# Attention steps written out instead of looped, normalizer arithmetic moved off VectorE, and the first fold of ctx moved up GpSimd's queue

## The reference

```python
def _autocorrelation(Q, K, V):          # H = 8 heads, Q = layernorm(x), K = V = ctx
    qf = jnp.fft.fft(q, axis=2)
    kf = jnp.fft.fft(k, axis=2)
    corr = jnp.fft.ifft(qf * jnp.conj(kf), axis=2).real
    topk = int(C * np.log(L))           # 12 of 512 lags, for each channel
    w, idx = jax.lax.top_k(corr.transpose(0, 1, 3, 2), topk)
    w = jax.nn.softmax(w, axis=-1)
    for i in range(topk):
        g = jnp.minimum(idx[:, :, None, :, i] + pos, L - 1)
        out = out + w[:, :, None, :, i] * jnp.take_along_axis(v, g, axis=2)
x = x + _L0_xattn_ref(_layernorm(x), ctx, ctx)
x = x + _L0_ffn_ref(_layernorm(x), A_w, B_w, Wq_w, keys)
```

## Time and profile before

| | |
|---|---|
| median of 3 runs | 2534.56 us (2531.9 to 2537.17) |
| the profiled execution's own time | 2531.53 us |
| its span, first to last instruction | 2529.7 us |
| mean granted clock of PE | 0.967 of full speed |
| busy share of the span: PE, DVE, POOL, ACT | 92%, 72%, 62%, 37% |

### The profile page before, as it was taken

One profiled execution on the slowest core, in us unless ns is written; L12 is line 12 of the kernel. 1 busy time (PEld: TensorE's weight loads), 2 busy tenths in 40 slices (PEclk: granted clock), 3 DMA queues, 4 the chain that ended last, 5 costly groups with the idle time before them and its releaser, 6 DMA issues.

```text
span 2529.7 us, 32161 instructions
## 1 busy us (share of the span) xinstructions
PE 2317.3 (92%) x9728; PEld 1570.1 (62%) x9728; DVE 1821.3 (72%) x3961; ACT 944.4 (37%) x1727; POOL 1566.1 (62%) x1004
## 2 busy tenths in 40 slices
PE   3799998998998998998999999659999999999999
PEld 1456654654654564554556566348787887878877
DVE  3888887887887887887988878745555565555552
ACT  2344443344433533443453443323333333233331
POOL 4878877886887887886878887523333333333330
PEclk7899999999999999998999999779999999999999
DMA  5233232222322322322231122444444444444431
GB/s 189 92 104 109 71 103 97 84 71 92 120 71 71 129 83 71 109 103 71 71 137 59 61 102 100 156 149 150 167 150 158 158 157 161 162 149 166 149 133 50
DMA packets 111452, 289.80 MB, mean 115 GB/s; under 512 B 7168, under 2 KB 7296, under 8 KB 110208
## 3 DMA queue, kind: packets, MB, share of 16 engines
q1 hardware_dynamic: 111360, 288.81, 32.4%
HBM read 221.68 MB, written 67.11 MB: 114 GB/s over the span
## 4 chain that ended last, share of the span: by engine, by line
PE 54%; POOL 25%; issue 11%; DVE 5%; DMA 2%; ACT 2%; POOLq 0%; SPq 0%; DVEq 0%; ACTq 0%
POOL r_f L1220 7%; PE z L495 5%; PE out L495 5%; PE out L497 5%; PE z L497 5%; PE out L496 5%; PE z L496 5%; PE evac L512 3%; PE pair L525 3%; POOL vf L1216 3%; POOL half_fold L1212 3%; PE evac L536 3%; POOL half_fold L1213 3%; PE evac L537 3%; PE lag L569 3%
## 5 line engine op out<-in xcount | busy, mean ns | idle before, releaser
L1255 POOL TENSOR_TENSOR rows<-rows,cin 128x1024 f32<-128x1024 f32 x48 | 114.5, 2386 | 410.0 <-DMA rows<-out_dram 284.6
L1220 POOL TENSOR_TENSOR r_f<-prod 128x1024 f32<-128x1024 f32 x128 | 305.9, 2398 | 81.7 <-DVE prod L798 80.0
L597 PE MATMUL pair<-r_f,back 128*128 128x512 f32 x768 | 334.8, 592 | 0.0
L597 PEld LDWEIGHTS pair<-r_f,back 128*128 128x128 f32 x768 | 145.8, 190 | 170.1 <-issue 168.4
L569 PE MATMUL lag<-lags,p_f 128*128 128x256 f32 x1024 | 233.2, 381 | 12.9 <-DVE e L819 12.9
L495 PE MATMUL pair<-w_hi,wts_hi 128*128 128x512 f32 x512 | 211.1, 412 | 17.0 <-DVE prod L798 16.6
L569 PEld LDWEIGHTS lag<-lags,p_f 128*128 128x128 f32 x1024 | 193.0, 191 | 39.9 <-issue 13.8
L495 PE MATMUL out<-b_hi,zt_hi 128*128 128x512 f32 x512 | 208.0, 406 | 1.5 <-ACT zt_hi L1168 1.5
L495 PE MATMUL z<-a_hi,xt 128*128 128x512 f32 x512 | 207.8, 406 | 0.0
L496 PE MATMUL pair<-w_lo,wts_hi 128*128 128x512 f32 x512 | 202.0, 395 | 0.0
L497 PE MATMUL pair<-w_hi,wts_lo 128*128 128x512 f32 x512 | 201.7, 394 | 0.0
(11 more groups left out here) (141 smaller groups left out, 5490.9 us busy)
## 6 DMA issues: line engine op xcount, KB each, us to landing
vf<-in_ctx_dram SPq DMA_DIRECT2D x32, 1024.0 KB, 5.1
xf<-in_x_dram SPq DMA_DIRECT2D x32, 1024.0 KB, 5.8
out_dram<-att_sb SPq DMA_DIRECT2D x32, 1024.0 KB, 5.1
rows<-out_dram SPq DMA_DIRECT2D x64, 512.0 KB, 3.7
cin<-out_dram SPq DMA_DIRECT2D x64, 512.0 KB, 3.9
xin<-in_x_dram SPq DMA_DIRECT2D x64, 512.0 KB, 4.0
out_dram<-rows SPq DMA_DIRECT2D x64, 512.0 KB, 2.6
stat_in<-in_x_dram SPq DMA_DIRECT2D x28, 1024.0 KB, 7.2
```

What stands on the lines that cost most here:

```text
L597: return nc.tensor.matmul(pair_ps[:, bank, :], back[:, 3 * bank + n, :], r_f[:, row, :], start=n == 0, stop=n == 2)
L1220: nc.gpsimd.tensor_tensor(dst, prod[:, slot, 0:2, :], prod[:, slot, 2:4, :], ALU.add).then_inc(add_done, 1)
L1255: nc.gpsimd.tensor_tensor(half, first, second, op).then_inc(c_added, 1)
```

## The change

- `steps` no longer makes a loop. The 33 steps are written out on each engine, with constants in place of registers in semaphore waits and addresses.
- The normalizer: DVE keeps the four L729 and the reciprocal. Its three small arithmetic instructions L731, L732 and L740 go. ACT does the first two as Identity and Copy ahead of its root, and POOL adds the 1.5 from an array of constants, in place of one multiplication.
- `fold_v` is cut in two. Its first instruction runs right behind `fold_x`, ahead of the four sums into `r_f`; the other three stay at the end of the step.
- The transposes of `turn_weights` go to other banks: block 1 to a bank of `pair` instead of the `evac` bank that DVE's second L807 frees, so that the wait for L807 stands at block 3.
- Between the two parts, `add_x(0, 0, 0)` moves from the end of step 31 to step 32, behind `fold_w`.

```diff
-        def steps(eng, body):
-            for r in (1, 2, 3):
-                body(-1, r, True, r > 1, True, True)
-            with eng.Fori(0, B - 2) as k:
-                for r in range(4):
-                    body(k, r, True, True, True, True)
...
+        def steps(body):
+            for i in range(GROUPS + 1):
+                k, r = (i - 3) // GPB, (i - 3) % GPB
+                body(k, r, i < GROUPS, i >= 1, i + 1 < GROUPS, k + 2 < B)
...
-            return evac_ps[l][:] if l < 2 else pair_ps[:, l, :]
+            return (evac_ps[0][:], pair_ps[:, 2, :], pair_ps[:, 3, :], evac_ps[1][:])[l]
...
                         if l == 0 and a:
                             pe.wait_ge(evac_act, 6 * i + 6)
                         elif l == 1 and a:
+                            pe.wait_ge(prod_ready, prod_x(i, 1) + 1)
+                        elif l == 1:
+                            pe.wait_ge(att_done, i - 1)
+                        elif l == 3 and a:
                             pe.wait_ge(evac_dve, 2 * i + 2)
-                        elif l == 2 and a:
-                            pe.wait_ge(prod_ready, prod_x(i, 1) + 1)
...
-                nc.vector.tensor_scalar(y[:, :, 0], mv[:, :, 1], EPS, -0.5, ALU.add, ALU.mult).then_inc(norm_step, 1)
-                nc.vector.tensor_scalar(mv[:, :, 0], mv[:, :, 0], -1.0, None, ALU.mult).then_inc(norm_step, 1)
...
-                nc.vector.tensor_scalar(mv[:, :, 1], y[:, :, 1], 1.5, None, ALU.mult).then_inc(norm_step, 1)
...
             def root(m):
-                act.wait_ge(norm_step, 8 * m + 5)
-                nc.scalar.activation(norm_x[1][:, :, 1], norm_x[1][:, :, 0], ACT.Sqrt, scale=-2.0).then_inc(root_done, 1)
+                mv, y = norm_x
+                act.wait_ge(norm_step, NORM_STEPS * m + LT)
+                nc.scalar.activation(y[:, :, 0], mv[:, :, 1], ACT.Identity, bias=consts[:, 0:1], scale=-0.5).then_inc(root_done, 1)
+                nc.scalar.activation(mv[:, :, 0], mv[:, :, 0], ACT.Copy, scale=-1.0).then_inc(root_done, 1)
+                act.wait_ge(root_done, 3 * m + 1)
+                nc.scalar.activation(y[:, :, 1], y[:, :, 0], ACT.Sqrt, scale=-2.0).then_inc(root_done, 1)
...
                 if f:
                     fold_x(i + 1)
+                    begin_fold_v(i + 1)
                 if b:
...
                     for n in range(4):
                         blk = W_BLOCKS[n]
                         add_products(prod_w(i, n), n % 2, r_f[:, 2 * blk:2 * blk + 2, :])
...
                 if f:
-                    fold_v(i + 1)
+                    end_fold_v(i + 1)
```

More of the change, by code:

```diff
@@ L288, in build_program @@
         NORM_OPS = 5
-        def steps(eng, body):
-            for r in (1, 2, 3):
-                body(-1, r, True, r > 1, True, True)
-            with eng.Fori(0, B - 2) as k:
-                for r in range(4):
-                    body(k, r, True, True, True, True)
[L298 to L301, removed]
+        NORM_STEPS = LT + 1
+        def steps(body):
+            for i in range(GROUPS + 1):
+                k, r = (i - 3) // GPB, (i - 3) % GPB
+                body(k, r, i < GROUPS, i >= 1, i + 1 < GROUPS, k + 2 < B)
         PARTS = 8
@@ L460, in first_parts @@
                 load_others(0, 1, 1)
-            steps(sp, body)
+            steps(body)
             for n in range(5, PARTS):
@@ L629, in body @@
                     out_row(3, 2).then_inc(pair_ready, 1)
-            steps(pe, body)
+            steps(body)
             def turn_tile(t, q):
@@ L728, in means @@
                 for j in range(LT):
-                    nc.vector.bn_aggr(mv[:, j, :], bn_x[:, j, :, :].rearrange("p g s -> p (g s)")).then_inc(norm_step, 1)
-                dve.wait_ge(norm_step, 8 * m + 4)
-                nc.vector.tensor_scalar(y[:, :, 0], mv[:, :, 1], EPS, -0.5, ALU.add, ALU.mult).then_inc(norm_step, 1)
-                nc.vector.tensor_scalar(mv[:, :, 0], mv[:, :, 0], -1.0, None, ALU.mult).then_inc(norm_step, 1)
+                    nc.vector.bn_aggr(norm_x[0][:, j, :], bn_x[:, j, :, :].rearrange("p g s -> p (g s)")).then_inc(norm_step, 1)
             def invert(m):
[L736 to L739, removed]
-                nc.vector.tensor_scalar(mv[:, :, 1], y[:, :, 1], 1.5, None, ALU.mult).then_inc(norm_step, 1)
+                dve.wait_ge(root_done, 3 * m + 3)
+                nc.vector.reciprocal(norm_x[1][:, :, 1], norm_x[1][:, :, 1]).then_inc(norm_step, 1)
             dve.wait_ge(start_loaded, 16 * GPB)
@@ L940, in body @@
                     choose_last()
-            steps(dve, body)
+            steps(body)
             def tile_step(u, k, r, a, b, f):
@@ L1152, in body @@
                     nc.scalar.activation(even_sb[:], pair_ps[:, 0:2, :], ACT.Copy).then_inc(even_copied, 1)
-            steps(act, body)
+            steps(body)
             def tile_step(u, k, r, a, b, f):
@@ L1238, in normalizers @@
                 pool.wait_ge(norm_ready, ready + 2)
-                nc.gpsimd.tensor_tensor(near, near, root, ALU.mult).then_inc(norm_ready, 1)
+                nc.gpsimd.tensor_tensor(near, near, consts[:, 1:1 + LT], ALU.add).then_inc(norm_ready, 1)
                 pool.wait_ge(norm_ready, ready + 3)
-                nc.gpsimd.tensor_tensor(rstd[:], near, mv[:, :, 1], ALU.add).then_inc(norm_ready, 1)
+                nc.gpsimd.tensor_tensor(rstd[:], near, root, ALU.mult).then_inc(norm_ready, 1)
                 pool.wait_ge(norm_ready, ready + 4)
@@ L1268, in body @@
                         fold_w(i - 1, t)
+                if is_step(i, GROUPS):
+                    add_x(0, 0, 0)
                 if a:
@@ L1281, in body @@
                         add_products(prod_w(i, n), n % 2, r_f[:, 2 * blk:2 * blk + 2, :])
-                if is_step(i, GROUPS - 1):
-                    add_x(0, 0, 0)
                 if is_step(i, GROUPS):
@@ L1289, in body @@
                 if f:
-                    fold_v(i + 1)
-            steps(pool, body)
+                    end_fold_v(i + 1)
+            steps(body)
             def tile_step(u, k, r, a, b, f):
```

17 lines of the change are left out of this document (11 added, 6 removed).

## The result

The changed kernel takes 2494.45 us, median of 4 runs (2492.05 to 2497.68), against 2534.26 us (2531.9 to 2537.17) of the kernel before in the same session: 0.9843 of its time, 95% interval 0.9826 to 0.986. The forecast was 2496 us. The profiled execution took 2492.05 us, with a span of 2490.2 us.

A forecast was written before the change was run, and what follows sets the result against it. A closed loop through att_sb and the transfers, 44.8 us, matches the step; the early fold makes it 47.6. Gains 36.3 + 2 + 1 - 1.4 - 0.6 = 37.3 us give 2494.2 or 2497.3, stated 2496 us, range 2470 to 2526.

The forecast's parts named there:

- The closed loop: From fold_x over sums, product 3, att_sb, store, loads and norm to the next fold_x: 44.8 us, 47.6 after the change.
- Rival B: The loop over att_sb is not closed, xf comes in time: steps of 45.2 us, 2438 us in all; chance 13%.
- No loop: Writing the steps out removes DVE's stalls on issue at five jumps: 5 x (56.6 - 45.7) = 54.5 us.
- rival D: Fetching written-out code stalls too, so the kernel gets slower; 2574 us with a stall in every second step; chance 7%.
- The normalizer: Without L731, L740 and L732 on DVE, its step falls from 51.1 us to a plain one and 0.2.
- The early fold: First fold of ctx ahead of POOL's sums: product 3 starts 4.82 + 2.4 = 7.2 us behind fold_x.
- The banks: Moved transposes remove PE's 0.4 us wait for L807: worth nothing in the 24 steps, up to 0.4 in others.
- Steps 27 to 30: Without stat_in 2 MB pass instead of 3, so the loop takes 44.9 us, against 45.3 before.
- PE's gaps: PE idles 3 us a step, before the forward transforms and at the fourth of L536/L537, waiting for v_neg.
- rival C: PE's clock falls to 0.94 with its gaps, steps of 48.8 us, 2525 us in all; chance 8%.
- The seams: Outside the 24 steps: start -1.4 and -0.6, steps 27 to 31 +2, between the parts +1 us.
- A: The forecast itself, 2496 us, with its own range of 2481 to 2511; chance 68%.

The follow-up runs named there:

- 4: The kernel before, loop and normalizer kept, with only the first fold of ctx moved ahead of the sums: 2552.89 us, ratio 1.0078.
- 8: The changed kernel with the second instruction of the fold of ctx also ahead of the four sums: 2560.89 us, ratio 1.011.
- (1): The changed kernel with the first fold of ctx back behind the four sums into r_f: 2444.08 us, ratio 0.9645 to the kernel before.
- experiment 7: The changed kernel with the load of stat_in issued ahead of the store of att_sb: 2438.56 us, ratio 0.9624 to the kernel before.
- (5): The changed kernel with the store of att_sb issued behind the load of xf: 2457.64 us, ratio 0.9704 to the kernel before.
- experiment 12: The kernel before with the steps written out on DVE alone, the loop kept on the other four engines: 2473.42 us, ratio 0.9761.
- (2): The kernel before with the steps written out on every engine and nothing else changed: 2470.73 us, ratio 0.9756.
- both corrections: The changed kernel with the load of stat_in ahead of the store and the first fold of ctx back behind the sums: 2429.75 us, ratio 0.9591.
- experiment 10: The kernel with both corrections, the transposes put back in their old banks: 2447.48 us, ratio 0.9658 to the kernel before.
- experiment 11: The changed kernel with the first add_x between the parts back at the end of step 31: 2496.83 us, ratio 0.9854.

## Why the prediction was right, step by step

**The closed loop** is the step on which everything hung, and it holds. Its four terms came out within 0.25 us each in the step shown, the step lengthened by most or all of an instruction's time when one was put in (experiments 4 and 8), and it shortened when one was taken out (1) or a megabyte was (7). Rival B, no closed loop, is refuted by the same four.

Two things in it were less well founded than they look. The prediction has only SP's queue and the transfers between `att_sb` and `norm`; that SP also waits for PE before it loads xf is missing, and with the store out of the way this second path held the step at 45.8 us (5). And the shortest way of 10.57 us was read in step 9, where `norm` did not wait for its load at all: it started at 529.87, when ACT was through with v_neg. So that row says nothing of the transfers, and that the way with the transfers came to 10.67 us was luck in part. The plain step came to 47.52 us on average, where 47.6 was taken.

**No loop: 54.5 us** by five times the difference of two rows. The changed kernel shows 53.0 for these steps, and the place was right: DVE alone (experiment 12). Made alone it gave 61.5 us of span, since the normalizer's steps came out shorter too (2). The Trainium skill (Runtime: NRT & Kernel Launch, Instruction fetch mechanics) says that a long kernel's instructions are streamed and that this is mostly hidden, while a taken branch is not. The traces agree on both: 24 written-out steps with one DVE wait on "issue" of 0.3 us, the five jumps with some 9.7. That fetching straight code stalls, rival D, is refuted.

**The normalizer: a plain step and 0.2 us.** Its steps take 48.78 us, 1.26 more than the mean plain step, and the ones behind it 46.32, 1.20 less. The two together are 95.10 us, against 95.04 for two plain ones: the normalizer costs next to nothing, as forecast. It only moves the mark by which I cut the steps, for POOL's five small instructions and their wait stand ahead of the last folds of ctx. Cut at the end of `fold_x` instead, the step with the normalizer that follows the one shown takes 47.46 us, from 540.96 to 588.42. DVE's reciprocal on norm_x takes 0.17 us, and of the two instructions moved to ACT the longer one 0.30 (ns):

```profile
L1020 ACT ACTIVATE norm_x<-norm_x,consts x8: 297/298/299, 30.6 to 1300.0; 128x4 f32<-128x4 f32 x8
```

What it cost before was read from one step, 51.1 us, and from that mark too; the mean of the six is 50.08. So the table's second and third lines are to be read as one: before, 107.00 us for the two steps, after, 95.10, where the forecast had 95.4.

**The early fold: 2.4 us on product 3.** Right, 7.32 us against 7.2. But product 2 waits 4.07 us, not about 2: the 2.4 us come on top of the 1.04 that it waited before, and DVE gets to it earlier.

**norm waits for the load in nearly all steps.** Right. The waits of ACT in the changed kernel, 200 to 1360 us:

```profile
ACT xf L1010 <- DMA xf<-in_x_dram: 54.9, 23, 3.6
```

**The banks: worth nothing in the 24 steps.** Not tried on the changed kernel itself. With both corrections made they are worth 0.63 us a step, not 0.4 (10).

**Steps 27 to 30: the loop with 2 MB, 44.9 us.** The number was met (44.86), but by luck: its reason is wrong. In none of these four steps does `norm` wait for the load of xf. ACT in one of them:

```profile
1425.49 0.60 ACT L1051 ACTIVATE v_neg<-evac 128x512 f32<-128x512 f32 x1 [2.17 <-PE evac L534]
1425.98 2.92 ACT L1010 ACTIVATE xf<-xf,shift,rstd 128x512 f32<-128x512 f32 x4
```

`norm` starts behind v_neg, on the third loop, as in experiment 7, whose steps are as long. With the early fold taken back (1) these steps take 44.62 us, so the fold costs 0.2 us here; the way down from 45.31 to 44.62 fits the 0.6 us of the banks in experiment 10.

**PE's gaps.** The wait for v_neg came at the fourth of the last forward transforms, in 18 steps, 0.8 us at most. One wait was not foreseen. The waits of PE in the changed kernel, 200 to 1360 us:

```profile
PE pair L492 <- DVE w_lo L881: 22.9, 24, 2.0
PE evac L533 <- DVE v_neg L796: 8.0, 18, 0.8
```

ACT makes w_hi behind its `norm`; with `norm` late, w_hi, DVE's w_lo and PE's first product of weights are late. It costs nothing in itself, as the loop is longer than PE's work. The clock stayed at 1.00 in 23 of the 24 steps, so rival C, a clock that falls in gaps of 3 us a step, is out.

**The seams.** Start -2.1 us (forecast -2.0), steps 27 to 31 +1.8 (+2), between the parts +1.9 (+1). The last was priced as 2.6 us won and 2 lost; experiment 11 shows 3.3 won on PE's wait and 2.3 in all. The loss was looked for on the wrong engine: the first L744 takes its 2.29 us, and it is POOL's `add_x` that takes 2.15 us longer (4.50 against 2.35). How 1 us of it is left in the end wasn't followed. The Trainium skill (SBUF — State Buffer, SBUF: two separate sides) says that two such instructions exclude each other and that the one that starts first is through before the other goes on. These two rows agree: 4.50 us is nearly the sum of 2.29 and 2.35.

**The chances.** A, B and C, which the prediction counts as faster, have 0.89 together and not 0.88.

## What to carry to other kernels

Before moving an instruction ahead of others on a queue, follow what is behind it all the way round: if the path comes back to its own start after one step, and is as long as the step, each instruction put into it costs its full time in every step. Such a path runs through DMA queues too. Here a store, a load that nothing needed soon and a load that the next step needed stood in one queue; taking the unneeded one out from between was worth 56 us and is free. When several such loops all have nearly one length, corrections don't add up (50 and 56 us alone, 65 together), so try them together before believing their sum.

## What the runs showed of the hardware

- A hardware loop's jump cost time on DVE alone, 9.6 to 9.8 us each; on four other engines it was hidden, to within 2.7 us in all. In a variant with three DVE instructions fewer in the loop the same jump cost some 6 us. What sets the size stays open.
- A 128 x 4 TENSOR_SCALAR on DVE that began while POOL ran one of its TENSOR_TENSORs of 2.4 us ended 0.02 to 0.04 us after it, whether 0.5 or 2.2 us of it were left. With POOL idle it took 0.17 us.
- DVE's L744 and POOL's `add_x`, begun 0.03 us apart, took 2.29 and 4.50 us, where alone they take 2.29 and 2.35.
- A wait of 0.41 us on PE between short groups of matmuls lengthened the step by 0.6 us, as the overlap of the groups is lost with it.
- The load of xf took 8.2 us from issue to landing behind two transfers of 1 MB, and 5.3 us behind one (medians): 2.9 us for a megabyte, near the 2.7 us by the 391 GB/s of the earlier trace rows.
